# Cross attention and a 16-expert FFN on one core: first chunk's attention on its own batch's keys, weight splits moved into chunk 0, halves, single transposes

## The reference

```python
q = layernorm(x) @ Wq + bq;  k = ctx @ Wk + bk;  v = ctx @ Wv + bv
x = x + softmax(where(mask, q @ k.T / 16, -inf)) @ v
f = layernorm(x)
scores = sigmoid(l2norm(f) @ l2norm(gate_w).T)          # 16 experts
combine = top 8 of scores, divided by their sum
routed = sum over e of combine[:, e] * ((silu(f @ w_gate[e]) * (f @ w_up[e])) @ w_down[e])
shared = (silu(f @ sw_gate) * (f @ sw_up)) @ sw_down
out = x + routed + shared
```

## Time and profile before

| | |
|---|---|
| median of 3 runs | 696.65 us (693.71 to 696.65) |
| profiled execution | 696.65 us, its span 694.8 us |
| TensorE | busy 97% of the span, granted clock 0.99 on average |
| VectorE, GpSimd, ScalarE | busy 64, 38 and 34% |
| DMA | 51.18 MB, 74 GB/s on average |
| first gate matmul | at 52.73 us |
| first down, second down | at 68.82 and 77.56 us |

### The profile page before, as it was taken

How to read it: one execution, slowest core, us unless ns; L and a number is a source line. 1 busy time by engine, 2 the same in 40 slices (tenths; PEclk the granted TensorE clock), 3 DMA queues, 4 the chain that set the end, 5 groups by cost and what they waited for, 6 DMA issues and landing times.

```text
span 694.8 us, 10881 instructions
## 1 busy us (share of the span) xinstructions
PE 675.7 (97%) x3995; PEld 586.7 (84%) x3995; DVE 446.1 (64%) x977; ACT 239.6 (34%) x485; POOL 262.8 (38%) x222
## 2 busy tenths in 40 slices
PE   7995899999999999999999999999999999999997
PEld 6574798888888889888888889888888888888886
DVE  4467656667576756677576756767566765765444
ACT  3545233333323233333333233233333234232221
POOL 2120532525343532525343432526344442434332
PEclk9999799999999999999999999999999999999999
DMA  6325511033110510023110510014100510005100
GB/s 190 114 59 151 181 61 41 22 96 119 62 31 0 184 61 32 32 77 138 61 31 1 184 62 31 30 50 166 61 31 1 184 60 32 1 21 195 61 0 31
DMA packets 32763, 51.18 MB, mean 74 GB/s; under 512 B 3918, under 2 KB 24391, under 8 KB 32711
## 3 DMA queue, kind: packets, MB, share of 16 engines
q1 hardware_dynamic: 32455, 50.23, 22.2%
...
q10 hardware_dynamic: 256, 0.26, 0.2%
...
## 4 chain that ended last, share of the span: by engine, by line
PE 92%; DMA 2%; DVE 2%; issue 1%; ACT 1%; SPq 1%; POOL 0%; POOLq 0%; DVEq 0%; ACTq 0%
PE y_ps L296 9%; PE gate_ps L296 9%; PE y_ps L297 9%; PE y_ps L298 9%; PE gate_ps L298 9%; PE gate_ps L297 9%; PE up_ps L298 9%; PE up_ps L297 9%; PE up_ps L296 9%; PE f_ps L405 2%; PE f_ps L384 2%; DMA x<-in_L_xattn_Wq_dram 1%; PE f_ps L413 1%; DMA cb<-c_rows 1%; PE up_ps L305 1%
## 5 line engine op out<-in xcount | busy, mean ns | idle before, releaser
L1135 POOL TENSOR_TENSOR hidden<-hidden,cb 128x512 f32<-128x512 f32 x128 | 200.7, 1569 | 290.4 <-DVE hidden L934 240.0
L930 DVE SCALAR_TENSOR_TENSOR hidden<-hidden,gate_ps 128x512 f32<-128x512 f32 x136 | 93.1, 685 | 149.9 <-ACT hidden L663 149.8
L663 ACT ACTIVATE hidden<-gate_ps 128x512 f32<-128x512 f32 x136 | 81.4, 599 | 262.1 <-PE gate_ps L298 261.5
L296 PE MATMUL y_ps<-W,hs 128*128 128x256 f32 x544 | 156.4, 288 | 7.0 <-issue 4.1
L297 PE MATMUL y_ps<-W,hs 128*128 128x256 f32 x544 | 152.5, 280 | 0.0
L298 PE MATMUL y_ps<-W,hs 128*128 128x256 f32 x544 | 152.3, 280 | 0.0
L940 DVE TENSOR_TENSOR hs<-hidden,hs 128x512 fp32r<-128x512 f32 x136 | 97.0, 713 | 29.3 <-ACT hs L670 29.3
L296 PEld LDWEIGHTS y_ps<-W,hs 128*128 128x128 f32 x544 | 103.1, 190 | 12.7 <-issue 4.8
L296 PE MATMUL gate_ps<-xT,W 128*128 128x512 f32 x272 | 108.4, 399 | 0.0
L298 PE MATMUL gate_ps<-xT,W 128*128 128x512 f32 x272 | 107.7, 396 | 0.0
L297 PE MATMUL gate_ps<-xT,W 128*128 128x512 f32 x272 | 107.4, 395 | 0.0
...
## 6 DMA issues: line engine op xcount, KB each, us to landing
cb<-c_rows SPq DMA_DIRECT2D x64, 512.0 KB, 4.5
xin<-in_x_dram SPq DMA_DIRECT2D x8, 512.0 KB, 3.6
out_dram<-x SPq DMA_DIRECT2D x7, 512.0 KB, 7.2
...
cb<-in_ctx_dram SPq DMA_DIRECT2D x1, 512.0 KB
...
```

Source lines behind the costliest of these rows:

```text
L296: mm(ps, lh, rh, start=first and i == 0, stop=False)
L663: af(ew[:, i, :], gate_ps[i][:], ACT.Tanh, scale=0.5).then_inc(tanh_done, 1)
L930: V_.scalar_tensor_tensor(out=ew[:, i, :], in0=ew[:, i, :], scalar=1.0, in1=gate_ps[i][:], op0=ALU.add, op1=ALU.mult).then_inc(silu_done, 1)
L1135: pg.tensor_tensor(h[:, i, :], ew[:, i, :], cb[:, pair % PLACES, (e - 1) % 2, :], ALU.mult) \
```

## The change

The places in the order of work, engine by engine ("c" is now the number of the chunk where "b, hf" stood).

The tables: LN statistics, deviation and scaling go in halves (two tiles) of a chunk, with a wait for each; a new piece add_bv stands in step 4. There is no SPLITS table, and keep_warm is 20 transposes at the start.

```diff
-DVE_AT = dict(ln1_stats=(1.5,), ln1_aggr=(1.5,), ln1_scale=(2.5, 2.5), maxes=(5.5, 6.5),
...
-POOL_AT = dict(add_bias=(1.5,), ln1_std=(2.5,), ln2_std=(9.5,), inverse_norm=(10.5,))
-
-SPLITS = dict(A0=range(0, 3), A1=range(3, 4), exps=range(4, 5), probs=range(5, 5), V3=range(5, 6),
-              t2_hi=range(6, 8), tanh_scores=range(8, 10), tanh1=range(10, 13), hidden=range(13, 15),
-              end=range(15, 17))
-WARM = {'start': 16, 'attend': 14, 'turn_ln2': 30, 'logits': 17, 'turn_z': 6}
-
+DVE_AT = dict(ln1=(1.5, 1.5), ln1_scale=(2.5, 2.5), maxes=(5.5, 6.5),
...
+POOL_AT = dict(add_bias=(1.5,), ln1_std=(2.5, 2.5), add_bv=(4.5, 4.5), ln2_std=(9.5, 9.5), inverse_norm=(10.5,))
+WARM = 20
```

```diff
-            for pair in range(PLACES):
-                spread(0, 0, pair)
...
+        POOL_SPLITS = (0, 1, 6, 8, 10, 12, 14, 16)
+        EARLY = 5
...
+            def move_v_tails():
+
+                sp.wait_ge(vt_split, 2)
+                for row, part in ((0, HI), (PAD, HI), (2 * PAD, LO)):
+                    for b in range(B):
+                        sp.dma_start(Vtail[row:row + PAD, b, :].bitcast(F32),
+                                     vt[b * PAD:(b + 1) * PAD, part, :].bitcast(F32)) \
+                            .then_inc(vt_loaded, 16)
...
+            for e in range(STAGES):
+                load_stage(e)
+            move_v_tails()
+            for e in range(STAGES, STAGES + 3):
+                load_stage(e)
+            load_x(1)
+            spread(0, 0)
+            spread(0, 1)
+            load_stage(STAGES + 3)
+            spread(0, 2)
+            spread(0, 3)
+            for e in range(EARLY + 2, NE):
+                load_stage(e)
+                if e % 2 == 0 and PLACES + (e - EARLY - 2) // 2 < PAIRS:
+                    spread(0, PLACES + (e - EARLY - 2) // 2)
+            for pair in range(PLACES + (NE - EARLY - 2) // 2, PAIRS):
```

```diff
-            project()
-            values(0)
-            pe.wait_ge(brow_scaled, 2)
-            pe.wait_ge(a_read, 4)
-            scores(0, 0, 0)
-            values(1)
-            scores(0, 0, 1)
-            values(2)
-            turn_p(0, 0, 0)
-            turn_p(0, 0, 1)
-            keep_warm("attend")
-            pe.wait_ge(v_lo, 2)
-            attend(0, 0, 0)
-            attend(0, 0, 1)
-            values(3)
-            turn_router()
-            keep_warm("turn_ln2")
-            turn_ln2(0, 0, 0)
-            turn_ln2(0, 0, 1)
-            keep_warm("logits")
-            pe.wait_ge(gate_split, 2)
-            logits(0, 0)
...
+            keep_warm()
+            turn_ctx_first()
+            keys_first()
+            turn_wq()
+            bias_row_first()
+            turn_x(0, 0)
+            keys_by_wq_first()
+            turn_ctx_rest(0)
+            turn_ctx_rest(1)
+            scores(0, 0)
+            turn_x(0, 1)
+            value_tails()
+            values(0, y_ps[:, 0, 0:D])
+            scores(0, 1)
+            turn_p(0, 0)
+            keys_rest(0)
+            turn_p(0, 1)
+            keys_rest(1)
+            attend(0, 0)
+            turn_router()
+            attend(0, 1)
+            values(1, y_ps[:, 0, 0:D])
+            bias_row_rest()
+            keys_by_wq_rest(0)
+            turn_ln2(0, 0)
+            turn_ln2(0, 1)
+            keys_by_wq_rest(1)
+            logits(0)
+            gate(0, 0)
+            turn_z(0)
+            up(0, 0)
+            gate(0, 1)
+            up(0, 1)
+            turn_c(0)
+            values(2, f_ps[:, 0, 0:D])
+            gate(0, 2)
+            up(0, 2)
+            for c in range(CHUNKS):
+                ahead = c + 1 < CHUNKS
+                for s in range(NE):
...
+            def keys_first():
+                pe.wait_ge(wk_loaded, 16)
+                pe.wait_ge(ctxT_read, 2)
+                for m in range(KD):
+                    for k in range(KD):
+                        ins = mm(y_ps[:, 1, m * KEYS:(m + 1) * KEYS], wk_in[:, k, m * P:(m + 1) * P],
+                                 ctxT[:, k, 0, 0:KEYS], start=k == 0, stop=k == KD - 1)
+                ins.then_inc(kt_made, 1)
...
+                    pe.wait_ge(vt_loaded, 16 * 3 * B)
...
+                turn(f_ps[:, 0, 0:TILES * 2 * E], zT[:, 0:P], ident[:]).then_inc(z_turned, 1)
+                turn(f_ps[0:TILES * E, 1, 0:P], cw.rearrange("p j e -> p (j e)"), ident[:]).then_inc(c_turned, 1)
```

```diff
+                af(ptail[2 * PAD:STACK, t], ptail[0:PAD, t].bitcast(F32), ACT.Copy).then_inc(p_hi, 1)
+                for j in range(TILES):
+                    ins = af(zT[j * 2 * E:(j + 1) * 2 * E, 0:P], f_ps[0:2 * E, 0, j * P:(j + 1) * P], ACT.Copy)
+                ins.then_inc(z_read, 1)
...
+            split_hi(3)
+            write_t2_hi(0, 0)
+            write_t2_hi(0, 1)
+            read_a_rest(0)
+            split_hi(4)
+            read_z(0)
+            tanh_scores(0)
+            tanh_gate(0, 0)
+            read_a_rest(1)
+            tanh_gate(0, 1)
+            combine_rows(0)
+            hidden_hi(0, 0)
+            write_v_hi(2, f_ps[:, 0, 0:D])
+            for c in range(CHUNKS):
...
+                    if c == 0 and s + EARLY < NE:
+                        split_hi(s + EARLY)
```

```diff
+                dve.wait_ge(x_biased, upto(c, 2, q + 1))
...
+            def ln_stats(src, first, done, c, q):
+                for j in js(q):
+                    ins = V_.bn_stats(stats[:, j, :], src[:, j, :])
+                ins.then_inc(bn_step, 1)
+                dve.wait_ge(bn_step, upto(c, 4, q + 1 if first else q + 3))
+                for j in js(q):
+                    ins = V_.bn_aggr(meanvar[:, j, :], stats[:, j, :])
+                ins.then_inc(done, 1)
...
+                    if c == 0 and s + EARLY < NE and s + EARLY not in POOL_SPLITS:
+                        split_lo(s + EARLY)
```

```diff
+            def split_lo(e):
+                pool.wait_ge(w_hi, e + 1)
+                pg.tensor_tensor(W[:, e, LO, :], stage[:, e % STAGES, :], W[:, e, HI, :].bitcast(F32),
+                                 ALU.subtract).then_inc(w_lo_pool, 1)
...
+            def add_bv(c, q):
+
+                if c == 0:
+                    pool.wait_ge(bv_loaded, 16)
+                pool.wait_ge(ln1_done, upto(c, 2, q + 1))
+                xh = xin[:, 2 * q:2 * q + 2, :]
+                pg.tensor_tensor(xh, xh, bvb[:].unsqueeze(1).broadcast_to([P, 2, D]), ALU.add).then_inc(x_biased, 1)
...
+            setup()
+            ln1_std(0, 0)
+            add_bv(0, 0)
+            ln1_std(0, 1)
+            add_bv(0, 1)
+            gate_norm()
+            split_lo(0)
+            ln2_std(0, 0)
+            ln2_std(0, 1)
+            split_lo(1)
+            inverse_norm(0)
+            weighted(0, 0)
+            for c in range(CHUNKS):
+                ahead = c + 1 < CHUNKS
+                for s in range(NE):
+                    if s + 1 < NE or ahead:
+                        weighted(c, s + 1)
+                    if c == 0 and s + EARLY < NE and s + EARLY in POOL_SPLITS:
...
+                    if c == 0 and s + EARLY < NE and s + EARLY in POOL_SPLITS:
+                        split_lo(s + EARLY)
```

1372 lines of the change are left out of this document (683 added, 689 removed).

## The result

| | before | after |
|---|---|---|
| median | 696.65 us (693.71 to 696.65) | **678.09 us** (677.08 to 678.86) |
| profiled execution, its span | 696.65, 694.8 us | 678.86, 677.0 us |
| gate(5) starts | 84.75 us | 63.51 us |
| from there to turn_x(2), about one chunk on | 81.67 us | 87.64 us |
| from turn_x(2) to the end | 528.4 us | 525.9 us |

The ratio is 0.9743 (95% interval 0.9714 to 0.9772). The forecast was 672.0, range 661 to 688. The three last rows of the table are read from starts of TensorE's rows (turn_x(2): 166.42 and 151.15 us) and the spans. turn_x(c) is the turning of chunk c's normalised x (tile xn) on TensorE, gate(e) and down(e) are the matmuls of expert e, and hs is the split hidden that down(e) reads.

What follows compares the result with a forecast made beforehand. TensorE's own work bounds the kernel behind 84.75 us, late expert-weight broadcasts the stretch ahead. Span 694.8 - 22.8 (prologue) - 3.4 (transposes) + 1.5 (splits) + 0 = 670.1 us, plus 1.85: 672 us, range 661 to 688.

Steps and rivals of the forecast that it cites:

- (c): Prologue: twelve value-tail copies from SP, all awaited by attend(0,0); 12 x 0.47 us issue and 1.6 us landing, to 29.6.
- (a): Prologue: the first loads, with bv behind them, take 13.8 us (bounds 11.5 and 15.5).
- (d): Prologue: attend, residual, LN, split_lo(1) at 2.2 us, expert 4's load and split, then read_z; turn_z at 44.0 us.
- (b): Prologue: add_bv, power, scalings, then transposes, values and scores at the low clock; the tails' halves exist at 22.4 us.
- (e): From turn_z to gate(5): TensorE is fed, 17.9 us of work; gate(5) at 62.0 against 84.75, -22.8 us.
- part 3: Chunk 0: 12 splits inside it fit on the other engines on average; +1.5 us (bounds 0 and 11).
- Part 2: turn_z and turn_c in seven later chunks: one transpose of 0.12 us for four taking 0.36; -3.4 us.
- Part 4: Steady chunks: LN halves and value bias add GpSimd work, taken to cost 0 us.
- B: Rival: chunk 0 stalls, six GpSimd splits each blocking VectorE by the shared-port lock rule; 683 us (to 687; half, 677); 17%.
- C: Rival: shorter prologue, the clock stays high and loads land at 11.5 us; 664 us (658 to 666); 14%.
- D: Rival: in steady chunks new GpSimd work delays a weighting, 4.5 us sticking out seven times; 703 us; 5%.
- E: Rival: loads of 12 experts and eight broadcasts share one queue, TensorE waits for each expert; 690 to 699 us; 4%.

Runs made afterwards that it cites:

- the best run: Changed kernel with value tails copied batch by batch, expert 7's load ahead of pair 2's cb transfers, expert 8's low part on VectorE: 667.06 us, ratio 0.9585.

## Why the prediction was right, and where not

The time, 678.1, is inside the range and 6 us above the figure; the form of the change's effect is the one forecast, a shorter prologue, and one term of the sum was mis-sized. That the time fell because the prologue got shorter is read from the rows of both kernels, and link (c) was tested by an edit; no run puts single pieces of the old order back, so how the 21.2 us divide among the moved pieces is not shown.

- **(a) to (d), the prologue.** bv lands 1.9 us sooner than the 13.8 taken, the tails' halves exist at about 19.9 in place of 22.4. In (b) the low clock did not hold: the granted clock from 10 to 24 us is 1.00, and eight value matmuls (15.65 to 17.38) took 0.22 us each where four at 0.5 were counted. The 0.22 us per transpose that (b) took for the low clock come from a stretch of the kernel before (1.59 to 5.26 us) whose granted clock reads 1.00 too. The twelve copies and their landing take 8.95 us in place of 7.2 (0.63 us each, where a load's issue takes 0.47), and attend starts at 28.8 for 29.6. Two errors of about 2 us each cancel. From attend to turn_z it is 14.5 us, forecast 14.4: split_lo(1) took 1.82 us, not 2.2. It also delayed xn by 1.5 us, which the sum did not have and which did not show: the second logits matmuls (41.26, 0.63 us) were done while ScalarE worked on expert 4's split (41.47), for whose load it had waited 1.04 us.
- **(e), gate(5) at 62.0.** It came at 63.5, so -21.2 in place of -22.8. 1.10 us is the wait for hs at down(2), behind GpSimd's split_lo(6): the first of the stalls that part 3 had to price. (In four runs with the same order there it is 0.30 to 0.33 us, in a fifth 1.01.) The other 1.1 us lie in small pieces along the list. cb was no bound: down(1) came at 59.37, without a wait (forecast 59.1).
- **Part 2, -3.4 us.** By the rows of the turns 0.69 us a chunk, -4.8; by the intervals between turns 0.5 to 0.7, -3.3 to -5.1; by medians -3.2 or -4.8. "One takes 0.12" is off by itself (it takes 0.06); that the sum was off is not shown.
- **Part 3, +1.5 us: the step that failed.** From gate(5) to turn_x(2) chunk 0 takes 87.64 us against 81.67, and with some 0.6 saved in it by the transposes that is 6.6 us. The forecast saw the place (the transposes of step 2) and named GpSimd's deviation as the cause; its sign "fewer than 2 us of TensorE waits" failed too (1.10 at down(2) and 3.3 at turn_x(1)). The deviation was ready at 67.18 us, when the first half of xn was just done. What held xn was GpSimd's weighting (0.98 us of the wait) and split_lo(8) (1.50 us). Close behind stood another cause: expert 7's load, issued behind cb transfers that wait for batch 3's values, with split_hi(7) and split_lo(7) ahead of xn. Each cured without the other leaves the stretch nearly as it was (-0.7 and +0.3 us, medians -2.7 and -1.6, the last not told from nothing); on the base with the tails by batch the load takes 1.7 us off the stretch and split_lo(8) a further 3.1. The low clock behind the waits, 0.83 from 60 to 80 us and 1.00 in the best run, is part of it.
- **Part 4, 0 us.** Shown for the two additions of the value bias. The halves of the deviations were not tried by themselves.
- **The sum with measured terms**, which must close and shows that no stretch is left out: 694.8 - 21.2 + 6.0 (81.67 to 87.64, with its transposes) - 2.5 (528.4 to 525.9) = 677.1 us of span, 677.0 measured.
- **The rivals.** B had the mechanism. That its price of half the six splits, 677, is near the time that came is luck: two of the six splits were seen to matter, 6 and 8, and of the 6.6 us lost split_lo(8)'s wait is 1.5; 1.8 are the other waits at turn_x(1), and in the rest is the low clock. On its rule: xn takes 0.70 or 0.73 us alone and 2.21 or 2.23 beside split_lo(1). The Trainium skill, "SBUF — State Buffer", Who interferes with whom, says that the second engine blocks until the first is done; the trace agrees where VectorE works from SBUF (hs at 59.96 us took 1.91 and ended 0.56 us behind split_lo(6)). In C the loads did land sooner, but the clock of 20 to 40 us was 0.74. D and E did not occur: behind turn_x(2) TensorE's waits come to 0.9 us in all, and of the loads in chunk 0 expert 7's is the only one that was seen to cost.
- **Not foreseen**: that the twelve copies need not all be awaited. Ordering them by batch brings 6.7 us, more than any stall cured in chunk 0.
